# Three-pass query, key and value products by batch halves, and the values' token shift as a transfer, in a two-layer network

## The reference

```
x = x + _layernorm(_L0_attn_ref(_layernorm(x), w_qkv, ...))

qkv = x @ w_qkv.T                       # 1024 query, 256 key, 256 value columns
q = qkv[..., :LATENT]
k = qkv[..., LATENT:LATENT + KV_DIM]
v_curr = qkv[..., LATENT + KV_DIM:LATENT + KV_DIM + half]
v_prev = qkv[..., LATENT + KV_DIM + half:]
v = concatenate([v_curr, pad(v_prev[:, :-1, :], ((0, 0), (1, 0), (0, 0)))], axis=-1)
q_pre, k_pre = (q, k)
q = causal_conv1d(causal_conv1d(q, qc1_w, qc1_b, 16), qc2_w, qc2_b, 1)   # 3 taps
k = causal_conv1d(causal_conv1d(k, kc1_w, kc1_b, 4), kc2_w, kc2_b, 1)
q = q + 0.5 * k_pre.mean(over heads);  k = k + 0.5 * q_pre.mean(over heads)
```

## Time and profile before

| | |
|---|---|
| Median of three runs | 2643.16 us (2641.68 to 2645.16) |
| Profiled execution, its own time | 2647.32 us |
| Its span, first to last instruction | 2645.5 us |
| Mean granted TensorE clock | 0.975 |
| Busy: TensorE, VectorE, GpSimd, ScalarE | 2461.3 (93%), 1780.5 (67%), 1489.6 (56%), 1430.1 (54%) us |
| First block of `attention` | from 0 to 136.4 us |
| Its TensorE groups: line 373, line 364, line 388 | 70.0, 26.9, 14.6 us busy |

### The profile page before, as it was taken

One profiled execution on the slowest core, in us unless ns is written; L12 is line 12 of the kernel. 1 busy time (PEld: TensorE's weight loads), 2 busy tenths in 40 slices (PEclk: granted clock), 3 DMA queues, 4 the chain that ended last, 5 costly groups with the idle time before them and its releaser, 6 DMA issues. The chain is left out here.

```text
span 2645.5 us, 37613 instructions
## 1 busy us (share of the span) xinstructions
PE 2461.3 (93%) x12784; PEld 1796.5 (68%) x12784; DVE 1780.5 (67%) x3192; ACT 1430.1 (54%) x2816; POOL 1489.6 (56%) x1274
## 2 busy tenths in 40 slices
PE   7989995888899699999999999999999999999967
PEld 3554443444687578878878878878878887787754
DVE  2163655676424786886887887777777778778765
ACT  2310004554222396686686686686676776776713
POOL 0062544454002257867767777678678677768642
PEclk9999997999899899999999999999999999999979
DMA  4022310000310343343343343253352352352300
GB/s 165 1 78 60 119 40 33 1 1 1 97 55 20 122 140 112 114 131 108 106 132 118 96 143 112 85 160 102 95 157 90 96 167 88 101 163 93 104 18 32
DMA packets 143630, 241.88 MB, mean 91 GB/s; under 512 B 28369, under 2 KB 48593, under 8 KB 143185
## 3 DMA queue, kind: packets, MB, share of 16 engines
q1 hardware_dynamic: 143440, 239.48, 28.9%
HBM read 232.08 MB, written 7.34 MB: 91 GB/s over the span
## 5 line engine op out<-in xcount | busy, mean ns | idle before, releaser
L1803 ACT ACTIVATE mix<-mix,sc 128x128 f32<-128x128 f32 x1024 | 310.8, 389 | 4.1 <-DMA sc<-head_scal 3.8
L2134 POOL TENSOR_TENSOR xend<-xdt,sc 128x384 f32<-128x384 f32 x128 | 106.7, 834 | 320.0 <-DVE xdt L1936 320.0
L1973 DVE SCALAR_TENSOR_TENSOR feat<-ps,chan,feat 128x511 f32<-128x511 f32 (+2 forms) x384 | 283.5, 738 | 1.8
L98 PE MATMUL ps<-xt_hi,w_in_hi 128*128 128x512 f32 x640 | 267.3, 418 | 12.9 <-ACT sg L1793 5.7
L1962 DVE TENSOR_TENSOR mix<-mix,cb 128x512 f32<-128x512 f32 x256 | 271.8, 1067 | 1.2 <-ACT mix L1809 1.2
L99 PE MATMUL ps<-xt_lo,w_in_hi 128*128 128x512 f32 x640 | 253.7, 396 | 0.0
L100 PE MATMUL ps<-xt_hi,w_in_lo 128*128 128x512 f32 x640 | 253.6, 396 | 0.0
L2150 POOL TENSOR_TENSOR w_in_lo<-w_in_raw,w_in_hi 128x512 fp32r<-128x512 f32 x158 | 211.5, 1339 | 61.3 <-ACT w_in_hi L1758 61.3
L2007 DVE TENSOR_TENSOR y_lo<-y,y_hi 128x512 fp32r<-128x512 f32 x128 | 183.8, 1436 | 81.4 <-ACT y_hi L1819 81.2
L1650 PE MATMUL ps<-w_o_hi,y_hi 128*128 128x512 f32 x512 | 207.7, 406 | 7.9 <-DVE y_lo L2007 4.3
L98 PE MATMUL ps<-xt_hi,w_g_hi 128*128 128x512 f32 x512 | 212.8, 416 | 2.2 <-DVE feat L1973 2.2
(11 more groups left out here) (290 smaller groups left out, 5905.6 us busy)
## 6 DMA issues: line engine op xcount, KB each, us to landing
mix<-row_cum SPq DMA_DIRECT2D x128, 512.0 KB, 5.6
w_in_raw<-in_w_conv_in SPq DMA_DIRECT2D x160, 256.0 KB, 3.1
w_g_raw<-in_w_gate_in SPq DMA_DIRECT2D x128, 256.0 KB, 3.3
ecb<-row_ecum SPq DMA_DIRECT2D x256, 96.0 KB, 3.3
w_o_raw<-in_w_out SPq DMA_DIRECT2D x64, 256.0 KB, 3.0
w<-in_w_c2q SPq DMA_DIRECT2D x16, 768.0 KB, 5.0
w<-in_w_c2q SPq DMA_DIRECT2D x16, 512.0 KB, 3.7
wqkv<-in_w_qkv SPq DMA_DIRECT2D x1, 3072.0 KB, 13.9
```

Of the source, the lines that this page charges most:

```text
L98: pe.matmul(out, a_hi, b_hi, start=(n == 0), stop=False)
L1803: last = act.activation(m, m, ACT.Relu, bias=sc[:, b, CUM, z, 2 * i + e:2 * i + e + 1], scale=-1.0)
L1973: dve.scalar_tensor_tensor(out=to, in0=ps[:, j % 2, 0:S - back], scalar=chan[:, bb % B, j, K1 - 1 - back:K1 - back], in1=to, op0=ALU.mult, ...
```

## The change

- The query, key and value products go in three fp32r passes. `xt` is replaced by `xt_hi` and `xt_lo` (in the storage of `q_tok`, without the column of zeros). ScalarE rounds each weight tile to `wqk_hi`, a ring of four; GpSimd subtracts it from the tile in place (`wqk_lo`).
- `w_qkv` is laid out in tiles of 128 columns, contiguous per partition, and loaded in twelve transfers of 256 KB, which stand between the loads of x and of the other weights. The first convolution's weights `w1` get a buffer of their own.
- The layer norm goes by batch halves, four tiles at a time: statistics and powers of four, turns into banks 4 to 7. The first product (m = 0, b = 0) stands on TensorE between the first and the second half's turns. On VectorE the order is: measure first half, aggregate it, measure second half, normalise first half, aggregate second half, low parts of the first half, normalise second half, low parts of it.
- `pre` is a ring of three.
- The values are one product of 256 columns per token tile. VectorE copies the first 128 columns to `v_tok` and the others, unshifted, to `v_prev`, which lies in `k_tok`. After the last copy SyncE moves `v_prev` to `v_tok` one token further: one transfer from partitions 0 to 126 to partitions 1 to 127 for all eight tiles, and for each batch one from partition 127 to partition 0 of the next tile; GpSimd has set the first token's row of each batch to zero. SyncE waits for the three before the block's end.

```diff
             def _(sp):
-                    for i in range(NT // 2):
+                    def load_x(i):
                         sp.dma_start(x[:, 2 * i:2 * i + 2, :],
                                      x_in[2 * i * P:(2 * i + 2) * P, :].rearrange("(t p) d -> p t d", p=P)).then_inc(x_loaded[i], 16)
-                    sp.dma_start(wqkv[:, :, :], w_qkv.rearrange("(k p) o -> p k o", p=P)).then_inc(wqkv_loaded, 16)
+                    def load_w(m):
+                        sp.dma_start(wqk[:, m, :, :], w_qkv[m]).then_inc(wqk_loaded[m], 16)
+                    load_x(0)
+                    load_x(1)
+                    load_w(0)
+                    load_x(2)
+                    load_x(3)
+                    load_w(1)
...
+                    sp.wait_ge(v_done, 2 * NT)
+                    sp.wait_ge(row_zero, 1)
+                    late_half = slice(KVD // 2, KVD)
+                    sp.dma_start(v_tok[1:P, :, late_half], v_prev[0:P - 1, :, :]).then_inc(v_shifted, 16)
+                    for b in range(B):
+                        sp.dma_start(v_tok[0:1, b * ZB + 1:(b + 1) * ZB, late_half],
+                                     v_prev[P - 1:P, b * ZB:(b + 1) * ZB - 1, :]).then_inc(v_shifted, 16)
+                    sp.wait_ge(v_shifted, 16 * (1 + B))
...
             def _(pool):
-                    norm_pool(pool, core, ln)
+                    def cut_low(m):
+                        pool.wait_ge(w_high, m + 1)
+                        pool.tensor_tensor(wqk_lo[:, m, :, :], wqk[:, m, :, :], wqk_hi[:, m % WR, :, :].bitcast(F32),
+                                           ALU.subtract).then_inc(w_low, 1)
+                    power(0)
+                    cut_low(0)
+                    power(1)
+                    for m in range(1, NA):
+                        cut_low(m)
...
             def _(dve):
-                    norm_vector(dve, core, ln, normed, x_loaded)
+                    measure(0)
+                    spread(0)
+                    measure(1)
+                    norm(0)
+                    spread(1)
+                    low(0)
+                    norm(1)
+                    low(1)
...
-                        dve.tensor_copy(v_tok[:, t, :], ps[:, t % 4, 0:KVD]).then_inc(v_done, 1)
+                        dve.tensor_copy(v_tok[:, t, 0:KVD // 2], ps[:, t % 4, 0:KVD // 2]).then_inc(v_done, 1)
+                        dve.tensor_copy(v_prev[:, t, :], ps[:, t % 4, KVD // 2:KVD]).then_inc(v_done, 1)
...
             def _(act):
+                    def cut_high(m):
+                        act.wait_ge(wqk_loaded[m], 16)
+                        if m >= WR:
+                            act.wait_ge(pre_ready, 2 * (m - WR + 1))
+                            act.wait_ge(w_low, m - WR + 1)
+                        act.activation(wqk_hi[:, m % WR, :, :], wqk[:, m, :, :], ACT.Copy).then_inc(w_high, 1)
...
             def _(pe):
-                            for k in range(KD):
-                                last = pe.matmul(ps[:, (2 * m + b) % 4, :], wqkv[:, k, m * P:(m + 1) * P],
-                                                 xt[:, k, b, 1:], start=(k == 0), stop=(k == KD - 1))
+                            if m == 0:
+                                pe.wait_ge(xt_low, (b + 1) * ZB)
+                            pe.wait_ge(w_low, m + 1)
+                            cols = slice(b * S, (b + 1) * S)
+                            last = product(pe, ps[:, (2 * m + b) % 4, :], [
+                                (wqk_hi[:, m % WR, k, :], wqk_lo[:, m, k, :], xt_hi[:, k, cols], xt_lo[:, k, cols]) for k in range(KD)])
                             last.then_inc(pre_ready, 1)
+                            if m == 0 and b == 0:
+                                turn(1)
...
-                        for back in range(2):
-                            for k in range(KD):
-                                last = pe.matmul(ps[:, t % 4, back * P:(back + 1) * P],
-                                                 xt[:, k, b, 1 - back + z * P:1 - back + (z + 1) * P],
-                                                 wqkv[:, k, LAT + KVD + back * P:LAT + KVD + (back + 1) * P],
-                                                 start=(k == 0), stop=(k == KD - 1))
+                        last = product(pe, ps[:, t % 4, 0:KVD], [
+                            (xt_hi[:, k, cols], xt_lo[:, k, cols], wv_hi[:, k, :], wv_lo[:, k, :]) for k in range(KD)])
```

More of the change, by code:

```diff
@@ L211, in keep @@
             return outer.enter_context(nc.sbuf_tensor(name, shape, dt))
+        with ExitStack() as same:
+            xt_hi = same.enter_context(nc.sbuf_tensor("a_xt_hi", [P, KD, B * S], F32R))
+            xt_lo = same.enter_context(nc.sbuf_tensor("a_xt_lo", [P, KD, B * S], F32R))
         q_tok = keep("q_tok", [P, NT, H0, HD])
@@ L246, in attention @@
             x_loaded = [core.sem(f"a_x_loaded{i}") for i in range(NT // 2)]
-            wqkv_loaded = core.sem("a_wqkv_loaded")
+            wqk_loaded = [core.sem(f"a_wqk_loaded{m}") for m in range(NA)]
+            wv_loaded = core.sem("a_wv_loaded")
+            w_high, w_low, xt_low, v_shifted, row_zero = (
+                core.sem("a_" + n) for n in ("w_high", "w_low", "xt_low", "v_shifted", "row_zero"))
             w1_loaded = core.sem("a_w1_loaded")
@@ L295, in _, with power @@
                     pool.wait_ge(half_set, 1)
-                    norm_pool(pool, core, ln)
+                    def power(b):
+                        tiles = slice(b * ZB, (b + 1) * ZB)
+                        pool.wait_ge(ln.vare, b + 1)
+                        pool.tensor_tensor(core.rstd[:, tiles], core.vare[:, tiles], core.half[:, 0:ZB], ALU.pow).then_inc(ln.rstd, 1)
+                    def cut_low(m):
+                        pool.wait_ge(w_high, m + 1)
+                        pool.tensor_tensor(wqk_lo[:, m, :, :], wqk[:, m, :, :], wqk_hi[:, m % WR, :, :].bitcast(F32),
+                                           ALU.subtract).then_inc(w_low, 1)
@@ L298, in _, with measure @@
+                    power(0)
[3 more added lines that the diff above has]
+                        cut_low(m)
+                    pool.wait_ge(w_high, NA + 1)
+                    pool.tensor_tensor(wv_lo[:, :, :], wv[:, :, :], wv_hi[:, :, :].bitcast(F32), ALU.subtract).then_inc(w_low, 1)
                 @blk.vector
                 def _(dve):
-                    norm_vector(dve, core, ln, normed, x_loaded)
+                    def measure(b):
+                        for t in range(b * ZB, (b + 1) * ZB):
+                            dve.wait_ge(x_loaded[t // 2], 16)
+                            dve.bn_stats(core.stats[:, t, :], x[:, t, :]).then_inc(ln.stats, 1)
@@ new lines, in spread @@
+                    def spread(b):
+                        for t in range(b * ZB, (b + 1) * ZB):
+                            dve.wait_ge(ln.stats, t + 1)
+                            dve.bn_aggr(core.mv[:, t, :], core.stats[:, t, :]).then_inc(ln.aggr, 1)
+                        tiles = slice(b * ZB, (b + 1) * ZB)
+                        dve.wait_ge(ln.aggr, (b + 1) * ZB)
+                        dve.tensor_scalar(core.vare[:, tiles], core.mv[:, tiles, 1], LN_EPS, None, ALU.add).then_inc(ln.vare, 1)
@@ new lines, in norm, with low @@
+                    def norm(b):
+                        dve.wait_ge(ln.rstd, b + 1)
+                        for t in range(b * ZB, (b + 1) * ZB):
+                            if t >= ZB:
+                                dve.wait_ge(ln.turned, t - ZB + 1)
+                            dve.tensor_scalar(normed[:, t % ZB, :], x[:, t, :], core.mv[:, t, 0:1], core.rstd[:, t:t + 1],
+                                              ALU.subtract, ALU.mult).then_inc(ln.normed, 1)
+                    def low(b):
+                        for t in range(b * ZB, (b + 1) * ZB):
+                            cols = slice(t * P, (t + 1) * P)
+                            dve.wait_ge(ln.xt, t + 1)
+                            dve.tensor_tensor(xt_lo[:, :, cols], ps[:, 4 + t % ZB, :].rearrange("p (k n) -> p k n", k=KD),
+                                              xt_hi[:, :, cols].bitcast(F32), ALU.subtract).then_inc(xt_low, 1)
@@ L350, in _, with turn @@
                     pe.wait_ge(ident_loaded, 16)
[L351 to L354, removed]
+                    def turn(b):
+                        for t in range(b * ZB, (b + 1) * ZB):
+                            pe.wait_ge(ln.normed, t + 1)
+                            if t >= ZB:
+                                pe.wait_ge(xt_low, t - ZB + 1)
+                            for k in range(KD):
+                                last = pe.transpose(ps[:, 4 + t % ZB, k * P:(k + 1) * P], normed[:, t % ZB, k * P:(k + 1) * P],
+                                                    core.ident[:, :])
+                            last.then_inc(ln.turned, 1)
+                    turn(0)
+                    pe.wait_ge(pads_zero, 3)
                     def conv1(pair):
@@ L363, in conv1 @@
```

(5 more changed lines are left out.)

57 lines of the change are left out of this document (41 added, 16 removed).

## The result

| | before | changed |
|---|---|---|
| Median | 2643.03 us (2640.9 to 2648.1) | 2650.43 us (2649.99 to 2651.18) |
| Profiled execution, own time | 2647.32 us | 2650.29 us |
| Its span | 2645.5 us | 2648.5 us |
| Next block of `attention` begins | 136.4 us | 142.4 us |

The changed kernel is slower by 7.4 us between the medians: ratio 1.0025, 95% interval 1.0015 to 1.0035. Forecast were 2651.8 us and a slower kernel.

A forecast was written before the change was run, and what follows sets the result against it. TensorE is busy in nearly every slice, but all engines wait at the block's end, there for the one-engine shift: block +7.6 us and clock 1.0 on 2643.2 give 2651.8 us, range 2626 to 2668.

The forecast's parts named there:

- Start by halves: Opening: normalising starts at 11.5 us instead of 13.36, the first product at 17.1, the second at 26.4.
- Products: Products in three passes: 2.80 us each against 3.47; with 21.5 of convolutions the piece ends at 101.1 us, not 112.84.
- GpSimd as cover: Weight cutting during the products: 1.34 us of GpSimd per block, in each 5.6 us TensorE uses one up; costs nothing.
- Values: Value products behind the first products: 96 matmuls of 0.117 us, 11.2 us, ending at 113.0, 15.0 us earlier.
- The shift: Block's end: 127-row transfer on one engine takes 30.1 us, freeing SyncE at 143.7, 7.6 us after the old 136.14.
- Idle clock: Behind the block's end: TensorE idle some 25 us, then a lower granted clock, adding 1.0 us (between 0 and 4).
- Sum: Whole kernel: block's end +7.6 us and clock 1.0 make 8.6 more, median 2651.8 us.
- Rival (a): Shift at the block's end: transfer dealt over sixteen engines, end at 121.1, time 2628.2 us; chance 0.22.
- Rival (b): Shift at the block's end: a few engines; two give an end at 129.5 and 2636.6 us; chance 0.08.
- Rival (c): Shift at the block's end: one engine, dearer packets of 42 ns, 14.2 us more, 2666 us; chance 0.1.

The follow-up runs named there:

- 112 and 15 rows: Changed kernel with its 127-row transfer cut into rows 0 to 111 and 112 to 126; 2627.1 us, 0.9943 of the kernel before.
- two products ahead: Changed kernel with transfer cut in 112 and 15 rows, plus a second product behind the second half's turns; 2625.91 us, 0.9933 of the kernel before.
- the kernel with 122 rows: Changed kernel with its 127-row transfer cut into 122 and 5 rows; 2636.36 us, 0.9976 of the kernel before.
- the 127 packets of 4 KB: Changed kernel with the 127 rows sent in one 4 KB run each into a dead buffer; 2644.68 us (one run).

## Why the prediction was right

By its steps:

- **Start by halves.** Normalising 11.5 predicted, 11.26 measured; first product 17.1 and 17.04; second product 26.4 and 25.01. Of the 1.4 us 1.1 are the first product, taken at the slow pace of the later stage's row, 5.26 us; half of it ran at 0.43 us a matmul and half at 0.23, 4.17 in all. Turns to last low part 3.7, predicted 4.0.
- **Products.** From the second product's start 19 of 2.80 us and the rest. The values' first matmul is at 101.22 after 0.69 us of idle, so the piece ends at 100.5, predicted 101.1. The rest was 22.3, not 21.5: 0.8 of the switches between products and convolutions was counted as product, because I divided a merged row by its count (0.434 us a record, where neighbours start 0.429 apart). It cancels half of the first product's gain.
- **GpSimd as cover.** A cut took 1.53 us on average, predicted 1.34; TensorE waited for none.
- **Values.** 0.119 us a matmul of 256 columns (94 steps from 101.45 to 112.60), predicted 0.117. With a first step of 0.23 all eight tiles took 11.6 us for 11.2. V = 112.81, predicted 113.0.
- **The shift.** Issue 113.43, predicted 113.6. One engine, as taken on the ground that 127 has no divisor. From the issue to the next block 29.0 us, predicted 30.4. Two errors stand against each other here. The packets follow at 25.7 ns, not 28, which takes off 2.3 us; the rest, from the issue to the first packet (1.47) and from the last one's end to the next block (1.24) with the small packets between, is 2.9 and not 2.0. And the 28 ns were read wrongly: a share of the engines' time over a count of packets gives the mean time of one packet and not their pace. By that measure the shift's packets take 31 ns, more than the identity's, but they overlap. Next block 142.40, predicted 144.0 (143.7 and the 0.3 of the meeting).
- **Idle clock.** I had added 1.0 us for the longer idle time. The granted clock was 0.81 and 0.50 in the idle stretches shown above, but the first key rows of the next block took 4.66 us against 4.42 before: 0.2. Behind them nothing can be laid on it (see the sum).
- **Sum.** Block +6.0 us for a predicted +7.6, median +7.4 for +8.6. The profiled spans differ by only 3.0: 6.0 of the block, 2.0 more from its end to the first scores (303.0 us for 301.0), 4.9 less in the attention stage and 0.1 less behind it. The long idle time doesn't explain the 2.0, for the kernels with the new opening in which the shift is hidden take from 300.4 us (112 and 15 rows) to 303.0 (two products ahead) over the same stretch. So against the medians the block explains 6.0 us of 7.4, and where the other 1.4 are is open; the single runs of before spread by more. That 2650.4 lies within 1.4 us of 2651.8 is therefore in part luck: the sum had 7.6 for the block and 1.0 for the clock, and the runs give 6.0 and 0.2.

Rival (a), sixteen engines, was priced at 2628.2 us; the kernel that deals the rows over sixteen and fifteen has 2627.1. Rival (b), two engines, at 2636.6; the kernel with 122 rows has 2636.4. In both profiles the next block begins 1.7 to 2.0 us before its forecast (119.72 for 121.4, 127.85 for 129.8), so these close hits owe something to luck too. Rival (c), dearer packets, fell: they came at a faster pace.

## What to carry to other kernels

Count the rows of a transfer before its bytes: 127 rows moved 0.5 MB in 26 us on one engine, and cutting off 15 of them hid it completely. A tile of 128 rows shifted by one partition leaves 127, so cut it into a multiple of 16 and a rest. And put a transfer whose end must be awaited at a meeting of all engines against what else is late there (here 7.5 us), not against the work it replaces.

## What the runs showed of the hardware

- SyncE's issue of the next small transfer took 23.9 us while the large one ran on one engine, at a mean share of the engines of 0.07 to 0.08; the issue behind the 122 rows took 10.3 us, that behind the 127 packets of 4 KB 8.5 us. Behind 112 rows it took 1.0 to 2.2 us.
- The first product's pace in the opening changed from 0.43 to 0.23 us a matmul at different places in different profiles (4.17, 4.33 and 4.72 us for twelve matmuls), and was the faster one throughout in others (2.88), which is worth up to 1.8 us and hides edits of that size. The granted clock is 1.00 in the rows of all these stretches, so it doesn't explain the pace; the cause is open.
- The attention stage took 221.2 to 229.8 us on the same instructions in ten kernels, with a granted clock of 0.94 to 0.85 in 120 us of it.
